# Quantisers without a square pass, halves of a quantiser apart, and the passage between two loops rewritten

## What is computed

```python
def _layernorm(x, axis=-1, eps=1e-05):
    m = jnp.mean(x, axis=axis, keepdims=True)
    v = jnp.var(x, axis=axis, keepdims=True)
    return (x - m) / jnp.sqrt(v + eps)

def rmsnorm(x, g):
    return x * jax.lax.rsqrt(jnp.mean(x * x, axis=-1, keepdims=True) + EPS_NORM) * g

def activation_quant(x):
    scale = 127.0 / jnp.maximum(jnp.max(jnp.abs(x), axis=-1, keepdims=True), EPS_Q)
    return jnp.clip(jnp.round(x * scale), -128, 127) / scale

def weight_quant(w):
    scale = 1.0 / jnp.maximum(jnp.mean(jnp.abs(w)), EPS_Q)
    return jnp.clip(jnp.round(w * scale), -1, 1) / scale

# h = bitlinear(x, w_in, g_in); y = silu(gate) * up; bitlinear(y, w_out, g_out)
# bitlinear: activation_quant(rmsnorm(x, g)) @ weight_quant(w).T
```

## Time and profile before

| | us |
|---|---|
| median of 3 executions | 1161.88 |
| lowest, highest | 1160.49, 1165.47 |
| the profiled execution | 1159.48 |
| its span on the core | 1157.7 |
| between span and time | 1.8 |

### The profile page before, as it was taken

The page is one execution under the profiler, slowest core; times in us unless marked ns, Lnnn a source line. Parts: engine busy times, 40 slices in busy tenths (PEclk is TensorE's granted clock), DMA queues, the critical chain, the costliest instruction groups (busy, mean ns, idle before and its releaser), DMA issues.

```text
span 1157.7 us, 31414 instructions
## 1 busy us (share of the span) xinstructions
PE 1023.5 (88%) x9700; PEld 785.5 (68%) x9733; DVE 852.6 (74%) x2737; ACT 741.3 (64%) x2097; POOL 365.6 (32%) x1096
## 2 busy tenths in 40 slices
PE   3768999999999999999999998999998887999995
PEld 2546676666666666666666666666666676888884
DVE  2367888888888888888888888888887543555553
ACT  2347777777777777777777777777776431333331
POOL 2012333433333333333333334333333211222222
PEclk9989999999999999999999999999999998999998
DMA  6541111111111111111111111111111403222221
GB/s 226 147 138 35 34 48 40 40 40 40 40 40 57 43 47 45 40 40 40 40 40 46 40 40 40 40 40 46 52 45 43 113 13 133 54 60 59 55 60 38
DMA packets 74291, 65.70 MB, mean 57 GB/s; under 512 B 39373, under 2 KB 63728, under 8 KB 74128
## 3 DMA queue, kind: packets, MB, share of 16 engines
q1 hardware_dynamic: 64832, 49.58, 14.7%
q0 software_dynamic: 3680, 9.38, 2.3%
q10 hardware_dynamic: 5744, 6.29, 1.9%
HBM read 36.57 MB, written 28.95 MB: 57 GB/s over the span
## 4 chain that ended last, share of the span: by engine, by line
issue 31%; DVE 19%; PE 15%; ACT 13%; POOL 12%; DMA 5%; SPq 3%; POOLq 1%; DVEq 0%; ACTq 0%
PE bank_a L593 7%; DMA rel_skew<-rel_scores 3%; POOL routed L563 2%; ACT vBD L942 2%; DMA rel_scores<-rel_tok 2%; PE bank_f L593 2%; PE bank_b L593 2%; ACT kBD L942 2%; DVE max L1320 2%; DVE o L1334 2%; ACT rel_tok L942 2%; POOL rstd_a L523 2%; ACT f_in L1084 1%; PE bank_b L596 1%; POOL rstd_f L523 1%
## 5 line engine op out<-in xcount | busy, mean ns | idle before, releaser
L1255 DVE SCALAR_TENSOR_TENSOR conv_lo<-xT_lo,c_taps,conv_lo 128x248 f32<-128x248 f32 x192 | 89.6, 466 | 16.3 <-ACT conv_hi L995 16.3
L1200 ACT ACTIVATE e_tanh<-bank_a 128x512 f32<-128x512 f32 x34 | 20.3, 597 | 103.5 <-PE bank_a L593 103.5
L593 PE MATMUL bank_a<-c_wo,oT 128*128 128x192 f32 x384 | 70.0, 332 | 7.4 <-ACT oT L942 7.4
L593 PE MATMUL bank_a<-e_xT,w_now 128*128 128x128 f32 x544 | 69.5, 281 | 5.8 <-DVE e_gate L1548 1.4
L593 PE MATMUL bank_a<-c_wv,a_xT 64*64 64x384 f32 (+1 forms) x512 | 74.2, 504 | 0.0
L593 PEld LDWEIGHTS bank_a<-e_xT,w_now 128*128 128x128 f32 x544 | 63.9, 193 | 14.8 <-issue 12.1
L593 PE MATMUL bank_a<-a_xT,c_wq 64*128 64x128 f32 (+1 forms) x512 | 71.7, 282 | 0.8 <-ACT a_xT L942 0.8
L593 PEld LDWEIGHTS bank_a<-c_wo,oT 128*128 128x128 f32 x384 | 61.5, 190 | 15.0 <-ACT oT L942 15.0
L593 PE MATMUL bank_b<-c_wqkv,b_xT 128*128 128x288 f32 x128 | 39.6, 432 | 34.7 <-ACT b_xT L942 34.6
L593 PE MATMUL bank_a<-a_xT,c_wk 64*128 64x128 f32 (+1 forms) x512 | 69.5, 282 | 0.0
L593 PEld LDWEIGHTS bank_a<-a_xT,c_wq 64*128 64x128 f32 (+1 forms) x512 | 64.3, 191 | 5.1 <-ACT a_xT L942 1.3
(11 more groups left out here) (268 smaller groups left out, 3138.4 us busy)
## 6 DMA issues: line engine op xcount, KB each, us to landing
rel_scores<-rel_tok SPq DMA_DIRECT2D x32, 492.0 KB, 2.6
rel_skew<-rel_scores SPq DMA_DIRECT2D x64, 124.0 KB, 3.1
x_tok<-in_x SPq DMA_DIRECT2D x32, 187.5 KB
e_rest<-routed SPq DMA_DIRECT2D x34, 97.0 KB, 1.9
e_tok<-routed SPq DMA_DIRECT2D x34, 96.0 KB, 1.9
routed<-pad_rows SPq DMA_DIRECT2D x8, 386.0 KB, 3.7
w_sb<-in_w ACTq DMA_DIRECT2D x2, 1152.0 KB, 8.0
w_sb<-in_w ACTq DMA_DIRECT2D x2, 1024.0 KB, 6.2
```

The lines of the kernel that those rows point to most:

```text
L593: return nc.tensor.matmul(dst, lhsT, rhs, start=start, stop=stop)
L1200: nc.scalar.activation(e_tanh[:, :], pa0[:, :], ACT.Tanh, scale=0.5).then_inc(e_tanhr, 1)
L1255: c.mark(v.scalar_tensor_tensor(conv_lo[:, :, :], xT_lo[:, :, k:k + PAIRS], c_taps[:, 0, k:k + 1], conv_lo[:, :, :], ALU.mult, ALU.add))
```

## The change

1. The mean square of `f_in` is no longer summed. `f_square_x` is gone from ACT; POOL computes it as the variance of `res_f` times `rstd_a` squared (two products), adds epsilon, takes the root, and multiplies by 1/127 (`quant_step`): five operations in place of three for x, and four in place of three for y.
2. DVE's quantiser is in two halves. `f_gain_x` and `f_gain_y` multiply by the gain alone and take the largest magnitude; `f_quantise_x` and `f_quantise_y` (`unit_of`) then make the unit, its reciprocal, and a new product of that with `rstd`. In the list each gain half stands directly ahead of its other half.
3. `ternary_weights` is called in `t_pool` of tile 1, a body earlier. Three `load_early` DMAs are issued later, behind stages of tile 0's attention.
4. Padding: three blocks in place of two, placed after tile 29; tile 30's scatter waits for them. The three step counts are read after the unrolled expert bodies. SP waits for the scatters only at its first load of rows. 33 fills in place of 38.

```diff
+PADDED_AT, PAD_BLOCKS = TILES - 3, 3
             for j in range(E_PEELED):
                 body({name: j - late for name, late in lag.items() if j >= late})
+            total, last, last_but_one = (
+                eng.value_load(plan[0:1, STEPS + k:STEPS + k + 1], min_val=TILES - 1 - k, max_val=MAX_TILES - k) for k in range(3))
             with eng.Fori(E_PEELED, total) as j:
...
-            sp.wait_ge(r_scattered, 16 * TILES)
-                if not first(j):
+                if first(j):
+                    sp.wait_ge(r_scattered, 16 * TILES)
+                else:
                     sp.wait_ge(e_xpose, j)
...
+            def rms_tail(k, m, done):
+                pool.wait_ge(var_eps[k], 4 * m + done)
+                pool.tensor_tensor(out=var[k][:, :], in0=var[k][:, :], in1=c_eps[:, 1:2], op=ALU.add).then_inc(var_eps[k], 1)
+                pool.wait_ge(var_eps[k], 4 * m + done + 1)
+                after_previous(pool, qsc_ready[k], m)
+                pool.tensor_tensor(out=rstd[k][:, :], in0=var[k][:, :], in1=half[:, :], op=ALU.pow).then_inc(var_eps[k], 1)
+                pool.wait_ge(var_eps[k], 4 * m + done + 2)
+                pool.tensor_tensor(out=step[k][:, :], in0=rstd[k][:, :], in1=magic[:, 2:3], op=ALU.mult).then_inc(rstd_ready[k], 1)
+            def f_inv_sqrt_x(m):
+                pool.wait_ge(shift_ready["a"], m + 1)
+                pool.tensor_tensor(out=var["x"][:, :], in0=mv["a"][:, 1:2], in1=rstd["a"][:, :], op=ALU.mult).then_inc(var_eps["x"], 1)
+                pool.wait_ge(var_eps["x"], 4 * m + 1)
+                pool.tensor_tensor(out=var["x"][:, :], in0=var["x"][:, :], in1=rstd["a"][:, :], op=ALU.mult).then_inc(var_eps["x"], 1)
+                rms_tail("x", m, 2)
...
-                if isinstance(m, int) and m == TILES - 1:
+                if isinstance(m, int) and m == PADDED_AT + 1:
                     pool.wait_ge(pads_written, 16 * NE)
...
-            fill_bank(38)
+            fill_bank(33)
...
-            def f_square_x(m):
-                act.wait_ge(a_out, m + 1)
-                nc.scalar.activation(f_sq[:, 0:D], f_in[:, :], ACT.Square, accum_out=ssq["x"][:, :]).then_inc(var_ready["x"], 1)
...
+                after_previous(dve, rstd_ready["x"], m)
                 v.tensor_tensor(res_f[:, :], hold_a[:, :], pa1[:, 0:D], ALU.add).then_inc(a_yread, 1)
...
+            def largest(c, k, src, gain, work):
+                c.link(v.tensor_tensor(work, src, gain, ALU.mult))
+                v.tensor_reduce(amax[k][:, :], work, axis=AX.X, op=ALU.max, apply_absolute_value=True).then_inc(amax_ready[k], 1)
+            def unit_of(c, m, k):
+                dve.wait_ge(amax_ready[k], m + 1)
                 dve.wait_ge(rstd_ready[k], m + 1)
-                c.link(v.scalar_tensor_tensor(work, src, rstd[k][:, :], gain, ALU.mult, ALU.mult))
-                c.link(v.tensor_reduce(amax[k][:, :], work, axis=AX.X, op=ALU.max, apply_absolute_value=True))
-                c.link(v.tensor_scalar(unit[k][:, :], amax[k][:, :], EPS, 1.0 / 127.0, ALU.max, ALU.mult))
-                v.reciprocal(qsc[k][:, 0:1], unit[k][:, :]).then_inc(qsc_ready[k], 1)
+                c.link(v.tensor_scalar(unit[k][:, :], amax[k][:, :], step[k][:, :], EPS / 127.0, ALU.mult, ALU.max))
+                c.link(v.reciprocal(inv_unit[k][:, :], unit[k][:, :]))
+                v.tensor_tensor(qsc[k][:, 0:1], inv_unit[k][:, :], rstd[k][:, :], ALU.mult).then_inc(qsc_ready[k], 1)
```

More of the change, by code:

```diff
@@ L124, in audio_tower @@
         half = sb("half", [P, 1])
[L125 removed]
+        magic = sb("magic", [P, 3])
         c_eps = sb("c_eps", [P, 6])
@@ L237, in audio_tower @@
         shift = {k: lp(f"norm_shift_{k}", [P, 1]) for k in ("t2", "a", "f", "b")}
-        ssq = {k: lp(f"ssq_{k}", [P, 1]) for k in ("x", "y")}
+        ssq = {"y": lp("ssq_y", [P, 1])}
+        step = {k: lp(f"quant_step_{k}", [P, 1]) for k in ("x", "y")}
+        inv_unit = {k: lp(f"inv_unit_{k}", [P, 1]) for k in ("x", "y")}
         qsc_ready = {k: sem(f"quant_scale_ready_{k}") for k in ("x", "y")}
@@ L324, in staggered @@
             eng.wait_ge(planned, 1)
-            total, last, last_but_one = (
-                eng.value_load(plan[0:1, STEPS + k:STEPS + k + 1], min_val=TILES - 1 - k, max_val=MAX_TILES - k) for k in range(3))
             def body(steps):
@@ L980, in t_copy_x @@
                 last.then_inc(t_xT, 1)
-                if now(m, 1):
-                    load_early(0, w1, slice(0, P), slice(0, P))
                 if now(m, 2):
@@ L1025, in a_bias_qw @@
                 last.then_inc(a_qwr, 1)
-                if now(m, 0):
-                    load_early(2, w2, slice(P, D), slice(KB, P))
             def a_copy_k(m):
@@ L1035, in a_copy_k @@
                 last.then_inc(a_kr, 1)
-                if now(m, 0):
-                    load_early(2, w1, slice(P, D), slice(0, KB))
                 if now(m, 1):
@@ L1059, in a_expo @@
                 nc.scalar.activation(p0[:, :, 0:T], p0[:, :, 0:T], ACT.Exp).then_inc(a_exp, 1)
+                if now(m, 0):
+                    load_early(0, w1, slice(0, P), slice(0, P))
             def a_copy_probs(m):
@@ L1063, in a_copy_probs @@
                 copy(pT0[:, :, :].rearrange("p h t -> p (h t)"), pa2[:, :]).then_inc(a_ptr, 1)
+                if now(m, 0):
+                    load_early(2, w1, slice(P, D), slice(0, KB))
             def a_copy_heads(i, src, ready):
@@ L1069, in stage @@
                     copy(oT0[:, lo:hi, :].rearrange("p c t -> p (c t)"), src[:, 0:(hi - lo) * P]).then_inc(ready, 1)
+                    if i == 0 and now(m, 0):
+                        load_early(2, w2, slice(P, D), slice(KB, P))
                 return stage
@@ L1279, in t_pool @@
                                 axis=AX.X, op=ALU.max).then_inc(t_pooled, 1)
+                if isinstance(m, int) and m == 1:
+                    ternary_weights()
             def t_moments(m):
@@ L1346, in a_residual, with f_gain_x @@
                 moments(c, "a", res_f[:, :])
[L1349 to L1355 removed]
+            def largest(c, k, src, gain, work):
[3 more added lines that the diff above has]
+                dve.wait_ge(amax_ready[k], m + 1)
+                dve.wait_ge(rstd_ready[k], m + 1)
+                c.link(v.tensor_scalar(unit[k][:, :], amax[k][:, :], step[k][:, :], EPS / 127.0, ALU.mult, ALU.max))
+                c.link(v.reciprocal(inv_unit[k][:, :], unit[k][:, :]))
+                v.tensor_tensor(qsc[k][:, 0:1], inv_unit[k][:, :], rstd[k][:, :], ALU.mult).then_inc(qsc_ready[k], 1)
+            def f_gain_x(m):
+                ch["f"].stage("gain_x", m)
+                dve.wait_ge(a_out, m + 1)
+                after_previous(dve, f_xqr, m)
+                largest(ch["f"], "x", f_in[:, :], c_gin[:, :], f_x[:, :])
             def f_quantise_x(m):
[L1358 to L1359 removed]
                 ch["f"].stage("quantise_x", m)
[L1361 removed]
                 after_previous(dve, dq_ready["x"], 3 * m)
[L1363 removed]
+                unit_of(ch["f"], m, "x")
             def f_silu(m):
@@ L1374, in f_silu, with f_gain_y @@
                                        ALU.mult).then_inc(f_yr, 1)
+            def f_gain_y(m):
+                ch["f"].stage("gain_y", m)
+                dve.wait_ge(f_yr, m + 1)
+                largest(ch["f"], "y", f_y[:, :], c_gout[:, :], f_gate[:, :])
             def f_quantise_y(m):
```

65 lines of the change are left out of this document (27 added, 38 removed).

## The result

The changed kernel takes 1156.56 us (median of five executions, 1155.39 to 1158.28), the kernel before 1164.53 (five, 1160.49 to 1168.84): ratio 0.9932, interval 0.9905 to 0.9958. That is 8 us less, where 24 were forecast (1137.5, range 1129 to 1147). The profiled execution took 1155.39 us, its span 1153.3.

The account below looks back on a forecast made before the run. It took the ring from PE's `a_output` through DVE, POOL and ACT's `b_xT` back to PE to bound the loop. Loop -10.2, start -7.5, passage -6.6 gave -24.3 us: median 1137.5, range 1129 to 1147.

Parts of the forecast that it names:

- R1: Loop: DVE's chain through `rot_c`, `q_rot` and `k_rep` leaves only 0 to 0.2 us a body; time 1144.8; chance 0.22.
- R4: Loop: `quant_step_x` becomes late on POOL, the loop loses 1.1 us a body; time 1169.5, slower; chance 0.03.
- the ternary weights and what hangs on them: Start: `ternary_weights` fits DVE's idle 8.49 us, so PE no longer stands 5.42 us for `f_xq`; taken as -5.9 us.
- the loads: Start: three `load_early` DMAs moved from beside the first write of `rel_scores`; -1.2 us, ends 0 and -2.8.
- Should they reach the second write, +1: Start: the three moved `load_early` DMAs might meet the second write of `rel_scores`, costing 1 us.
- The -1.0 for y's first wait: Start: DVE's 1.95 us wait for `rstd_y` in y's first use shrinks by some 1.0 us, with the gain half under it.
- (a): Passage: the earlier padding ends about when tile 30's scatter is ready, more likely 3 us before; cost 0 to 0.5 us.
- (b): Passage: ACT's wait for tile 30's scatter shrinks, -1.5, PE's low clock goes, -0.7; tile 29's scatter is delayed, +0.8.
- (c): Passage: from `planned` to the first `e_tok` issue SP needs 4.2 us; only the address stays, some 0.9 us: -3.3.
- (d): Passage: with 33 fills PE's clock stays at 2.4 GHz in the first expert step: -1.6 us.
- (e): Passage: the three step counts now stand ahead of PE's loop, 1.8 us of its sequencer, partly under products: +1.0 us.
- (f): Passage: the second quantiser's wait goes where the last tile is alone: -1.3 us.

Follow-up runs that it names:

- the experiment with the short row: Changed kernel with POOL's five operations ahead of the x unit cut to two, so x gets a wrong unit: body 26.89 us, ratio 0.9858.
- the third profile: The changed kernel as it is, run and profiled a third time: ratio 0.9929 to the kernel before, body 27.20 us.

## Why the prediction was wrong, by its steps

**The loop: -10.2 forecast, +1.7 found.** The first link that it names is right (`b_xT` moves up by 0.48, forecast 0.36 to 0.49). Three steps fail behind it.

1. "`k_rep` ends at 508.88 now and would end no earlier ... PE loses some 0.1 us." This was mis-sized. PE takes q 8.76 us behind `res_f`, `k_rep` ends at 8.49, and in the change, where PE waits for `k_rep`, it goes on 0.06 us behind its end: the slack is 0.2 us or so. If `k_rep` ends no earlier, PE can keep 0.2 of the 0.49 and loses the rest in one place; this is an estimate from those rows, and no run shows just that case. The rows for it were at hand. Nor was it true that `k_rep` can't end sooner: with POOL's x operations first it ends at 8.18, and PE keeps the whole 0.48 at q. Taken out of the kernel before, the square was worth 0.11 us, and none of it at q; with the change's other orders it was worth nothing.
2. "`quant_step_x` would be there at about 506.2, covered by 0.4 us." In that body's time it ended at 506.8. I started POOL's row earlier because it no longer waits for the sum. It doesn't wait, it stands in line: `norm_shift_b` ends at 4.23 us behind `res_f`, and the row starts at 4.19, where it started at 4.09. Two more operations follow, three of the five drawn out (0.43, 0.30, 0.81 against 0.19, 0.19, 0.55). Price 0.31 us a body, by the experiment with the short row.
3. "`q_rot` may be held 0.14 us longer." `hold_a` moved by 0.5 us, off `q_rot` (0.51 to 0.36) and onto `k_rep` (0.35 to 0.74). Price 0.22 us a body. By the rule of the Trainium skill ("SBUF — State Buffer", section "Who interferes with whom") a DVE instruction with two SBUF inputs contends with a GpSimd instruction that reads SBUF. `q_rot` and `k_rep` agree with it, 0.35 or 0.36 us alone and 0.51 to 0.75 beside `hold_a`. Of POOL's short operations one lay beside such an instruction and wasn't drawn out (`norm_shift_b`, 0.19 us at 504.32 in the kernel before, beside `conv_hi`). And the rule prices nothing until one knows who meets whom: the sum took the old victim at the new time.

So R1 had the place (DVE's row up to `k_rep`, though not the loss) and R4 the trigger, a late `quant_step_x`. R4 was given 0.03 because it had to lose 1.1 us a body; the lesser form, in which it only eats the gain, was in no case. The bounds (2.9 to 14.2) excluded a loss for no reason in the rows. The loop is +0.15 us in plain bodies but +0.05 in the mean: fewer bodies are stretched by the read-back of the relative scores. That it has 0.15 us more time to land in would explain this; no run tests it.

**The start: -7.5 forecast, -5.3 in the means** (bounds -5 to -9.5; the first pair of profiles alone shows -1.4). The terms as given add up to -7.8, not -7.5. Ternary weights run from 43.50 under the first tile's attention, PE's wait for `f_xq` fell from 5.42 to 0.75:

```profile
72.89 0.39 PE L614 MATMUL bank_f<-ident,f_xq 128*128 128x128 bf16 x2 [0.75 <-ACT f_xq L1121]
...
80.43 1.10 PE L611 MATMUL bank_a<-rel_skew,ident 128*128 128x496 f32 x2 [1.70 <-DMA rel_skew<-rel_scores]
```

That is PE's timeline of the first profile. The terms themselves came true or better: the ternary weights and what hangs on them gave 6.2 to 7.3 us from one `res_f` to the next where nothing came between (27.5 us for 33.7 and 34.8), against 6.6 in the sum, and the loads 1.0 us at like clock, against 1.2. What failed is the step "Should they reach the second write, +1", which the sum took in by 0.3 at most: it happened in one of the three profiles, where the start ran at the full clock, and the trip cost 3.5 us. The -1.0 for y's first wait gave nothing by itself: PE no longer waits 0.86 us for `f_yq`, but then 1.04 us for `p`. The rest is the chance of the low clock ahead of tile 0's `res_f`, 11.4 us in the mean of the change's profiles and 8.6 before: in the first profile of the change

```profile
54.00:64.00 10.00, 8.08 (x57) 6.75 (x56) 2.20 (x8) 4.85 (x13) 1.39 (x5) 0.52 0.99 274
```

the granted clock is at 1.2 GHz for nearly all of ten microseconds, with PE busy for eight of them; `a_output` takes 4.04 us for 2.19.

**The passage: -6.6 forecast, -4.1 in the means.** ACT's waits, SP's rows, DVE's plan and PE's first steps, in the first profile of the change, answer to the earlier trace rows:

```profile
938.33 0.36 ACT L960 ACTIVATE moe_row<-res_m 128x192 f32<-128x192 f32 x1 [1.71 <-DMA routed<-moe_row,slot_now]
...
957.82 0.36 ACT L960 ACTIVATE moe_row<-res_m 128x192 f32<-128x192 f32 x1 [4.16 <-DMA routed<-moe_row,slot_now]
```

```profile
933.64 11.88 SPq L451 DMA_DIRECT2D routed<-pad_rows  x8
968.13 0.37 SPq L463 DMA_DIRECT2D e_tok<-routed  x1
```

```profile
967.18 0.20 DVE L1564 CAST plan<-plan_f 128x83 int32<-128x83 f32 x1
```

```profile
970.24 0.41 PE L614 MATMUL bank_t<-ident,e_tok 128*128 128x128 f32 x2 [0.88 <-DMA e_tok<-routed]
971.51 2.93 PE L611 MATMUL bank_a<-e_xT,w_now 128*128 128x128 f32 x16 [0.86 <-ACT e_xT L960]
```

- (a) right: no engine waits for the padding.
- (b) wrong: -1.4 forecast, about 0 found. The scatter of tile 29 now flies beside three blocks of padding, ACT waits 1.71 us for it (1.30 and 2.53 in the other two), and `b_project` of the last tile starts 29.1 to 30.5 us behind `res_f` where it was 28.1. I had put +0.8 on that, and it is 0.9 to 2.3; it takes what the shorter wait before 957.82 gives. Not all of it is the padding's doing: with the padding put back ACT doesn't wait there, and `b_project` still starts at 29.7; why stays open.
- (c) right: from the plan's end to `e_tok` 0.75 us for 4.18, -3.4. But it hangs on the padding's move as well: with the padding back it was 2.31.
- (d) right in two of three: the first step's products take 2.05 us in the third profile, 2.93 in the first. The idle time ahead doesn't tell them apart: 0.88 us in the first, 0.97 in the third.
- (e) right: the third step comes 5.9 to 6.0 us behind the second and not 4.9, for the step counts, as PE's timeline of the third profile shows:

```profile
975.99 2.02 PE L611 MATMUL bank_a<-e_xT,w_now 128*128 128x128 f32 x16 [1.41 <-DVE e_gate L1577]
...
981.98 2.02 PE L611 MATMUL bank_a<-e_xT,w_now 128*128 128x128 f32 x16 [1.20 <-issue]
```

- (f) wrong: where the last tile is alone, DVE is busy with other rows until y's product, and the wait was 0.21 us, not 1.3.

## What to carry to other kernels

An operation taken off one engine's row is worth no more than the slack at the next meeting with a row that doesn't move up too: look for that meeting (here PE's transposition and `k_rep`) and read how long one had waited for the other. When work goes to an in-order engine, its start is where that engine's row has room, not where its input is ready, and every later instruction of that row lies beside other instructions of DVE than before, and may draw them out: set its order anew with the change. Loads that are moved out of one transfer's way have to be followed to the next one.
